# Layer-2 weight, bias and 12 of 16 row tiles loaded inside nucleus step 1, the first group summed and measured in its tail, and the onward stage in another order

## The chip, the cores and the metric

The kernel runs on one core of one Trainium2 chip. The metric is the device time of one execution in microseconds, and lower is better. Engines are named as in the profile: PE (TensorE matmuls), PEld (its weight loads), DVE (VectorE), ACT (ScalarE), POOL (GpSimd) and SP (SyncE, which here only issues DMAs; SPq is its queue).

## What is computed

Four pre-normalised graph layers over 2048 nodes with 256 features, all on one weighted adjacency matrix. The change touches the place between layer 1 and layer 2.

```python
h = relu(layernorm(x));  x = x + L0(h, adj)    # 8-head attention masked and biased by adj
h = relu(layernorm(x));  x = x + L1(h, adj)    # two steps of diffusion and of nucleus (top-p) attention
h = relu(layernorm(x));  x = x + L2(h, adj)    # a_norm @ h @ W.T + b
h = relu(layernorm(x));  x = x + L3(h, adj)    # relu(adj_norm @ (h @ weight))

def L1(X, S, ...):                             # tail of layer 1
    Y = X + Z                                  # Z: the sum of the diffused and attended rows, weighted
    return (Y - mean(Y)) / sqrt(var(Y) + 1e-5) * gamma + beta

def L2(x, adj, W, b):
    deg = adj.sum(axis=1);  dis = (deg + 1e-8) ** -0.5
    return (dis[:, None] * adj * dis[None, :]) @ x @ W.T + b
```

## The kernel before, in words

The rows are held as 16 tiles of 128 partitions by 256 features. The program is a row of phases, written out by hand for each engine: `setup`, `adjacency`, `attend` (layer 0), then for the two steps of layer 1 `refresh` and `nucleus`, then `onward` and `last`. Between two phases stands a barrier of all engines, at which the phase's semaphores are cleared, so the next phase begins when the slowest engine of this one is done. Inside a phase each engine works down its own list and waits on semaphores. Nothing is scheduled by a planner.

`nucleus` for step 1 ends in `last_tiles` on PE: the products of the last four tiles (12 to 15), each followed by `after`, which turns one tile, multiplies it by a weight and adds it into `y` (ACT copies out). Beside this DVE runs the tail: when the first 12 tiles of `y` are ready, it takes `bn_stats` (L2480) and `bn_aggr` (L2483) of each, adds epsilon (L2485), and centres them and multiplies by gamma (L2487). POOL raises the result to the power of minus one half (L2029). SP loads the halves of the transposed adjacency (L1624, L1627) and has nothing left to do after the last of them.

`onward` (L964) makes layer 2's input. Its work goes in four groups ("quads") of four tiles, b = 0 to 3:

- SP loads the saved rows `x_d` (they already hold beta) into `add`, a group at a time (L996), between them layer 2's weight and bias (L998, L999), then layer 3's weight (L1000). It waits until all of that is there and only then issues the 16 loads of the transposed adjacency, 1 MB each (L1005), which `last` reads.
- DVE: `stats_of(0, 3)` measures the four tiles of `y` that the tail left out. `row_scales` makes row factors. `onto(b)` (L1115) multiplies a tile of `y` by its inverse deviation and adds it to `add`: that is x after layer 1. `stats_of(1, b)` (L1096 to L1102) measures it, POOL makes the power (L1014), `aim(b)` (L1122) makes the negative mean times the inverse deviation. `weights_in` (L1133, L1134) copies the turned weight and the broadcast bias out of PSUM. `remainder(b)` (L1128) makes the low halves.
- ACT: `normal(b)` (L1059) is the normalised and rectified group, `copy(b)` (L1066) brings the turned group out of PSUM, `cut(b)` (L1074, L1077) cuts the product into high half and rest. The order is normal(b), copy(b), cut(b-1).
- PE: it turns the weight (L1045) and broadcasts the bias (L1046), then `turn(b)` (L1027, eight transposes) and `products(b)` (L1036). The order is turn(b+1), products(b). Its first instruction waits for `w_loaded` at 48, which counts layer 2's weight, its bias and layer 3's weight.

`last` multiplies the adjacency tiles by the result (L1225) in 16 steps, each waiting for its own tile, then does layer 3 (L1258). The trace leaves numbers out of names: `l_w` is the weight of layer 2 (L1045) and of layer 3 alike, `l_b_row` is `l2_b_row`.

## Time and profile before

| | us |
|---|---|
| median of 3 runs | 3342.86 (3341.6 to 3344.99) |
| the profiled execution | 3342.79 |
| its span in the trace | 3341.0 |
| PE busy in the span | 2956.0 (88%) |
| DVE busy | 2162.7 (65%) |
| ACT busy | 1346.5 (40%) |
| end of `nucleus` step 1 (last ACT result) | 3087.97 |
| `onward`, from DVE's first to its last instruction | 3088.98 to 3147.39 |
| `last`, from PE's first product to the end | 3148.23 to 3341 |

The page sums busy time over the whole span, in which the engines' shares are averages over phases with different limits. For the stretch around the change the timeline of each engine is read instead: each row has the start, the duration from the first to the last of the merged instructions, and in brackets the idle time of the engine ahead of it with what ended it. Single windows of 0.5 us show TensorE's granted clock, as a share of 2.4 GHz.

### The profile page before, as it was taken

The numbers are of one execution on the slowest core, as the hardware profiler recorded it, in microseconds if no ns is written. First come the engines' busy times: TensorE is split into PE (matmuls) and PEld (weight loads), VectorE is DVE, ScalarE is ACT, GpSimd is POOL, SyncE is SP. The second block draws the span as 40 slices with busy tenths as digits, with TensorE's granted clock in tenths as the row PEclk, the third lists the DMA queues.
The fourth block names the chain that finished last, engine by engine and source line by source line (L and its number), as shares of the span: only waits on it lengthen the run. The fifth ranks groups of instructions, "written<-read, shape, count | busy, mean of one in ns | idle before, by whom it ended". The sixth has DMA issues, their size and how long they took to land. (4 is left out here: it accounts for less than half of the span.)

```text
span 3341.0 us, 56511 instructions
## 1 busy us (share of the span) xinstructions
PE 2956.0 (88%) x20632; PEld 2223.5 (67%) x20632; DVE 2162.7 (65%) x4426; ACT 1346.5 (40%) x1750; POOL 57.2 (2%) x70
## 2 busy tenths in 40 slices
PE   3989999999999999999999778878784668697699
PEld 3976776767767677676776447656563556575588
DVE  7866655556555565656556488888488887886331
ACT  5743434444344443344434323333316455522311
POOL 0000000000000000000000000000000000000100
PEclk7999999999999999999999989989987889899899
DMA  7938647466474664746647412100010010100500
GB/s 267 410 134 203 184 120 199 112 190 186 117 201 111 192 183 117 196 120 183 193 112 218 107 57 89 39 13 14 26 40 25 3 49 13 39 26 2 232 1 26
DMA packets 587858, 396.82 MB, mean 119 GB/s; under 512 B 538563, under 2 KB 553414, under 8 KB 562118
## 3 DMA queue, kind: packets, MB, share of 16 engines
q1 hardware_dynamic: 585990, 382.49, 38.5%
q10 hardware_dynamic: 1728, 12.58, 1.1%
q8 instruction: 73, 1.20, 0.1%
q14 instruction: 67, 0.55, 0.1%
HBM read 223.05 MB, written 37.75 MB: 78 GB/s over the span
## 5 line engine op out<-in xcount | busy, mean ns | idle before, releaser
L652 PE MATMUL av<-vw_hi,pT_hi 128*128 128x256 f16 x2048 | 559.7, 273 | 7.4 <-DMA pT_lo<-e_lo 7.4
L805 DVE SCALAR_TENSOR_TENSOR e_lo<-e,e_hi 128x2048 f16<-128x2048 f32 x128 | 293.2, 2291 | 420.7 <-ACT e_hi L716 414.7
L652 PE MATMUL av<-vw_hi,pT_lo 128*128 128x256 f16 x2048 | 559.9, 273 | 0.0
L652 PE MATMUL av<-vw_lo,pT_hi 128*128 128x256 f16 x2048 | 559.8, 273 | 0.0
L641 PE MATMUL logits<-kT_hi,qT_hi 128*128 128x512 f16 x1024 | 388.5, 379 | 0.6 <-DVE vT_lo L825 0.6
L641 PE MATMUL logits<-kT_hi,qT_lo 128*128 128x512 f16 x1024 | 388.1, 379 | 0.0
L641 PE MATMUL logits<-kT_lo,qT_hi 128*128 128x512 f16 x1024 | 388.1, 379 | 0.0
L710 ACT ACTIVATE att_small<-att_small,minus 128x1 f32<-128x1 f32 x128 | 37.6, 294 | 769.5 <-DVE att_small L800 769.5
L791 DVE CUSTOM_DVE_ANT_0 e<-logits,bias,att_small 128x1024 f32<-128x1024 f32 x256 | 328.3, 1282 | 0.6 <-issue 0.3
L2050 DVE SCALAR_TENSOR_TENSOR nuc_junk<-nuc_e,nuc_thr 128x2048 bf16<-128x2048 f32 x140 | 323.7, 2348 | 3.9
L711 ACT ACTIVATE e<-e,att_small,sc 128x2048 f32<-128x2048 f32 x128 | 266.2, 2080 | 0.0
L716 ACT ACTIVATE e_hi<-e 128x2048 f16<-128x2048 f32 x128 | 244.5, 1910 | 16.3 <-DMA pT_hi<-e_hi 1.0
L652 PEld LDWEIGHTS av<-vw_hi,pT_hi 128*128 128x128 f16 x2048 | 201.0, 98 | 44.4 <-issue 8.1
L652 PEld LDWEIGHTS av<-vw_lo,pT_hi 128*128 128x128 f16 x2048 | 200.9, 98 | 36.3
L652 PEld LDWEIGHTS av<-vw_hi,pT_lo 128*128 128x128 f16 x2048 | 200.9, 98 | 23.8
L1707 PE MATMUL nuc_l<-logit_k,logit_q 128*128 128x512 f32 x256 | 134.5, 677 | 64.1 <-ACT nuc_e L1902 57.1
L641 PEld LDWEIGHTS logits<-kT_hi,qT_lo 128*128 (+1 forms) x1024 | 100.2, 98 | 120.9
L641 PEld LDWEIGHTS logits<-kT_hi,qT_hi 128*128 (+1 forms) x1024 | 100.1, 98 | 118.7 <-issue 10.6
L641 PEld LDWEIGHTS logits<-kT_lo,qT_hi 128*128 (+1 forms) x1024 | 100.2, 98 | 106.6
L1683 PE MATMUL nuc_l<-nuc_u,nuc_xsT 128*128 128x256 f32 x320 | 90.6, 439 | 79.9 <-ACT nuc_xsT L1880 69.2
L384 PE MATMUL adj_tp<-ident_one,adj_rows 128*128 128x129 f32 x512 | 123.1, 405 | 30.5 <-DVE adj_count L420 30.5
L384 PEld LDWEIGHTS adj_tp<-ident_one,adj_rows 128*128 128x128 f32 x512 | 122.9, 337 | 30.7 <-DVE adj_count L420 30.7
(436 smaller groups left out, 5783.6 us busy)
## 6 DMA issues: line engine op xcount, KB each, us to landing
bias<-bias_scratch SPq DMA_DIRECT2D x130, 1024.0 KB, 4.8
bias_scratch<-adj_bias SPq DMA_DIRECT2D x16, 1024.0 KB, 8.5
adjT_scratch<-adjT SPq DMA_DIRECT2D x16, 1024.0 KB, 8.7
nuc_at_hi<-adjT_scratch SPq DMA_DIRECT2D x32, 512.0 KB, 3.8
nuc_at_lo<-adjT_scratch SPq DMA_DIRECT2D x32, 512.0 KB, 4.5
adjT<-adjT_scratch SPq DMA_DIRECT2D x16, 1024.0 KB, 20.0
adj_rows<-in_adj_dram ACTq DMA_DIRECT2D x12, 1024.0 KB, 8.9
adj_rows<-in_adj_dram SPq DMA_DIRECT2D x4, 1024.0 KB, 13.7
```

Source lines behind the costliest of these rows:

```text
L384: last = nc.tensor.matmul(o, rows_u[:, t // 2, t % 2 * P:(t % 2 + 1) * P], ident1[:, :], start=True, stop=True)
L641: last = nc.tensor.matmul(o, QT[w][:, k, ds(t * P, P)], KT[x][:, k, c0:c0 + BANK], start=(k == 0 and w == x == 0), stop=(k == 1 and w == 1))
L652: last = nc.tensor.matmul(AV[par], PT[par][w][:, m, :], VW[x][:, m, :], start=(m == 0 and w == x == 0), stop=(m == T - 1 and w == 1))
L710: nc.scalar.activation(masked(par), nb(par), ACT.Exp, bias=minus[:, 0:1], scale=1.0)
L711: nc.scalar.activation(E[par][:, :], E[par][:, :], ACT.Exp, bias=nb(par), scale=sc[:, 0:1], accum_out=ssum(par)).then_inc(exped, 1)
L716: nc.scalar.activation(EH[:, :], E[par][:, :], ACT.Copy, scale=P_SCALE).then_inc(hi_s, 1)
L791: return nc.vector.tensor_tensor_reduce(E[par][:, cols], L[half][:, :], B[par][:, cols], 1.0, (small[:, par, 6:7], m0(par))[half], ALU.add ...
L805: nc.vector.scalar_tensor_tensor(out=EL[:, :], in0=E[par][:, :], scalar=P_SCALE, in1=EH[:, :], op0=ALU.mult, op1=ALU.subtract).then_inc(lo ...
L1683: nc.tensor.matmul(WEIGHTED, xT[:, n * D + k * P:n * D + (k + 1) * P], U[:, n, k, :], start=(n == k == 0), stop=False)
L1707: last = nc.tensor.matmul(scores_in(i)[:, b * BANK:(b + 1) * BANK], QT[:, i * P:(i + 1) * P], KT[:, b * BANK:(b + 1) * BANK], start=True, ...
L2050: nc.vector.scalar_tensor_tensor(out=void[:, k % 2, :], in0=e[:, g % 2, k, 0:N], scalar=bound[:, k:k + 1], in1=e[:, g % 2, k, 0:N], op0=co ...
```

## The change

1. The buffers of layer 1's small weights become views of one tile `wbuf` of the same size, kept outside of the layer-1 block. `x_mv`, `x_rstd` and the semaphores `x_here` and `w2_here` move out too.
2. In `nucleus` step 1 SP, behind its last adjacency load, loads layer 2's weight into `wbuf` and the bias into the row of `gb` that held beta. It then loads the groups 0, 1 and 2 of `x_d`, each when `c_done` says that PE and ACT are done with the four tiles of `acc` that it overwrites.
3. The tail on DVE goes on: the sum of group 0, its statistics and the addition of epsilon. POOL gets a second power instruction.
4. In `onward` SP loads only the fourth group and layer 3's weight and then issues the 16 adjacency loads with no wait between. PE's first wait is for layer 2's weight and bias alone. The copies of `weights_in` move from DVE to ACT. On PE the order becomes products(b), turn(b+1). On ACT cut(b-1) now stands ahead of copy(b). On DVE `aim(0)` comes first, group 1 ahead of the statistics of `y`'s last four tiles and of `row_scales`, and `centre(3)` one group later.

```diff
@@ build
+            wbuf = sb(c, "small_weights", [P, 2 * D])
+            x_mv, x_rstd = sb(c, "x_mv", [P, T, 2]), sb(c, "x_rstd", [P, T])
+            ahead = (wbuf, gb, x_d, x_here, w2_here, x_mv, x_rstd, a["L2_gnn_W"], a["L2_gnn_b"])
@@ nucleus, SP
+                if step:
+                    sp.dma_start(wbuf[:, :].rearrange("p (k n) -> p k n", k=KC), w2_d.rearrange("(k p) n -> p k n", p=P)).then_inc(w2_here, 16)
+                    sp.dma_start(gb[0:1, 1, :], b2_d.rearrange("(a d) -> a d", a=1)).then_inc(w2_here, 16)
+                    for b in range(DONE // 4):
+                        sp.wait_ge(c_done, 4 * (b + 1))
+                        sp.dma_start(out[:, 4 * b:4 * b + 4, :], x_d[:, 4 * b:4 * b + 4, :]).then_inc(x_here[b], 16)
+                    sp.wait_ge(w2_here, 32)
+                    for b in range(DONE // 4):
+                        sp.wait_ge(x_here[b], 16)
@@ nucleus, POOL
+                    pl.wait_ge(x_asked, 1)
+                    nc.gpsimd.tensor_tensor(x_rstd[:, 0:4], x_rstd[:, 0:4], halfp[:, 0:4], ALU.pow).then_inc(tail_powed, 1)
@@ nucleus, DVE, behind the tail
+                    v.wait_ge(tail_powed, 1)
+                    v.wait_ge(x_here[0], 16)
+                    for t in range(4):
+                        nc.vector.scalar_tensor_tensor(out=out[:, t, :], in0=y[:, t, :], scalar=y_rstd[:, t:t + 1], in1=out[:, t, :],
+                                                       op0=ALU.mult, op1=ALU.add).then_inc(x_chain, 1)
+                    for t in range(4):
+                        v.wait_ge(x_chain, 4 + t)
+                        nc.vector.bn_stats(y_stats[:, t, :], out[:, t, :]).then_inc(x_chain, 1)
+                    v.wait_ge(x_chain, 8)
+                    for t in range(4):
+                        nc.vector.bn_aggr(x_mv[:, t, :], y_stats[:, t, :]).then_inc(x_chain, 1)
+                    v.wait_ge(x_chain, 12)
+                    nc.vector.tensor_scalar(x_rstd[:, 0:4], x_mv[:, 0:4, 1], LN_EPS, None, ALU.add).then_inc(x_asked, 1)
@@ onward, PE
-                pe.wait_ge(w_loaded, 48)
+                pe.wait_ge(w2_here, 32)
...
-                pe.wait_ge(copied_w, 2)
                 turn(0)
                 for b in range(QUADS):
+                    if b == 0:
+                        pe.wait_ge(copied_w, 2)
+                    products(b)
                     if b + 1 < QUADS:
                         turn(b + 1)
-                    products(b)
@@ onward, ACT
                 normal(0)
+                weights_in()
                 copy(0)
                 for b in range(1, QUADS):
                     normal(b)
+                    cut(b - 1)
                     copy(b)
-                    cut(b - 1)
```

On DVE, from the centring at the end of `nucleus` step 1 into `onward`, the order was this (`nuc_y_stats`, `deg` and `onw_mv` hold statistics, `acc` is `add`, `l_in` and `l_out` are the row factors, `l_wT` and `l_bias` the copies of `weights_in`):

```order
L2487 SCALAR_TENSOR_TENSOR y<-y,deg,gamma_beta 128x256 x12
L1616 UNCONDITIONAL_BRANCH
L1087 UNCONDITIONAL_BRANCH
L1144 MEMSET l_ones 1x128
L1096 BN_STATS onw_stats<-y 128x6 x4
...
L1142 TENSOR_SCALAR l_out<-l_out 128x16
L1115 SCALAR_TENSOR_TENSOR acc<-y,y_rstd,acc 128x256 x4
L1096 BN_STATS onw_stats<-acc 128x6 x4
L1099 BN_AGGR onw_mv<-onw_stats 128x2 x4
L1102 TENSOR_SCALAR onw_rstd<-onw_mv 128x4
L1133 COPY l_wT<-l_tp 128x512
```

In the changed program the same stretch reads:

```order
L2501 SCALAR_TENSOR_TENSOR y<-y,deg,gamma_beta 128x256 x12
L2507 SCALAR_TENSOR_TENSOR acc<-y,y_rstd,acc 128x256 x4
L2511 BN_STATS nuc_y_stats<-acc 128x6 x4
L2514 BN_AGGR x_mv<-nuc_y_stats 128x2 x4
L2516 TENSOR_SCALAR x_rstd<-x_mv 128x4
L1619 UNCONDITIONAL_BRANCH
L1095 UNCONDITIONAL_BRANCH
L1148 MEMSET l_ones 1x128
L1131 SCALAR_TENSOR_TENSOR onw_minus<-x_mv,x_rstd 128x4
L1123 SCALAR_TENSOR_TENSOR acc<-y,y_rstd,acc 128x256 x4
L1104 BN_STATS onw_stats<-acc 128x6 x4
```

The sum and the statistics of group 0 moved across the phase's end (the two branches), and `onward` begins with the small instruction that ACT's first group waits for.

On ACT, at the start of `onward`, the order was this (`y` is the normalised group, `onw_xT` the turned one, `h_hi` and `onw_rest` the cut product):

```order
L1059 ACTIVATE y<-acc,onw_minus,onw_rstd 128x256 x4
L1066 ACTIVATE onw_xT<-onw_tp 128x512 x2
L1059 ACTIVATE y<-acc,onw_minus,onw_rstd 128x256 x4
L1066 ACTIVATE onw_xT<-onw_tp 128x512 x2
L1074 ACTIVATE h_hi<-onw_u,l_in 128x256
L1077 ACTIVATE onw_rest<-onw_u,l_in 128x256
```

It now is:

```order
L1061 ACTIVATE y<-acc,onw_minus,x_rstd 128x256 x4
L1083 ACTIVATE l_wT<-l_tp 128x512
L1084 ACTIVATE l_bias<-l_bc 128x256
L1068 ACTIVATE onw_xT<-onw_tp 128x512 x2
L1061 ACTIVATE y<-acc,onw_minus,x_rstd 128x256 x4
L1076 ACTIVATE h_hi<-onw_u,l_in 128x256
L1079 ACTIVATE onw_rest<-onw_u,l_in 128x256
```

The two copies of the weight and the bias came in, and the second `onw_xT` moved behind the eight cuts.

On PE, in `onward`, the order of the transposes (`onw_tp`) and the products (`onw_u`) was:

```order
L1045 MATMUL l_tp<-ident,l_w 128x128 x4
L1046 MATMUL l_bc<-l_b_row,l_ones 128x256
L1027 MATMUL onw_tp<-ident,y 128x128 x16
L1036 MATMUL onw_u<-l_wT,onw_xT 128x256 x8
L1027 MATMUL onw_tp<-ident,y 128x128 x8
L1036 MATMUL onw_u<-l_wT,onw_xT 128x256 x8
L1027 MATMUL onw_tp<-ident,y 128x128 x8
L1036 MATMUL onw_u<-l_wT,onw_xT 128x256 x16
```

and is now:

```order
L1046 MATMUL l_tp<-ident,small_weights 128x128 x4
L1047 MATMUL l_bc<-gamma_beta,l_ones 128x256
L1028 MATMUL onw_tp<-ident,y 128x128 x8
L1037 MATMUL onw_u<-l_wT,onw_xT 128x256 x8
L1028 MATMUL onw_tp<-ident,y 128x128 x8
L1037 MATMUL onw_u<-l_wT,onw_xT 128x256 x8
```

followed by the same pair twice more. Each group's products no longer stand behind the next group's transposes.

## Rows read from the trace of the kernel before

**Rows 1.** The chain that ended last: start us, us, what.
```profile
3148.23 31.60 PE last_pr L1225 x288
...
3337.43 0.42 DVE acc L1342
```
**Rows 2.** Windows: us, busy by engine (count), granted clock, DMA share, GB/s.
```profile
3160.00:3341.00 181.00, 176.88 (x1558) 158.10 (x1556) 38.43 (x98) 26.51 (x56) 9.56 (x12) 1.00 0.04 13
```
**Rows 3.** Waits 3060 to 3160: engine, line, waited for: total us, times, longest.
```profile
ACT y L1059 <- DVE onw_minus L1122: 18.0, 4, 16.7
...
PE l_tp L1045 <- DMA l_w<-in_L_gnn_weight_dram: 11.9, 1, 11.9
```
**Rows 4.** DVE's timeline, end of `nucleus` and `onward`.
```profile
3080.28 4.83 DVE L2487 SCALAR_TENSOR_TENSOR y<-y,deg,gamma_beta 128x256 f32<-128x256 f32 x12
3088.98 0.17 DVE L1144 MEMSET l_ones<- 1x128 f32 x1 [3.87 <-PEq L127]
...
3091.82 0.17 DVE L1142 TENSOR_SCALAR l_out<-l_out 128x16 f32<-128x16 f32 x1
...
3102.74 1.66 DVE L1115 SCALAR_TENSOR_TENSOR acc<-y,y_rstd,acc 128x256 f32<-128x256 f32 x4
...
3104.51 1.40 DVE L1096 BATCH_NORM_STATS2 onw_stats<-acc 128x6 f32<-128x256 f32 x4
...
3106.36 0.17 DVE L1102 TENSOR_SCALAR onw_rstd<-onw_mv 128x4 f32<-128x4 f32 x1
...
3146.97 0.42 DVE L1128 SCALAR_TENSOR_TENSOR h_lo<-h_hi,onw_rest 128x256 f16<-128x256 f16 x1 [0.30 <-ACT onw_rest L1077]
```
**Rows 5.** ACT's timeline, end of `nucleus` and `onward`.
```profile
3087.59 0.38 ACT L1939 ACTIVATE y<-nuc_l 128x256 f32<-128x256 f32 x1 [1.65 <-PE nuc_l L1780]
3104.63 2.07 ACT L1059 ACTIVATE y<-acc,onw_minus,onw_rstd 128x256 f32<-128x256 f32 x4 [16.66 <-DVE onw_minus L1122]
3108.83 1.08 ACT L1066 ACTIVATE onw_xT<-onw_tp 128x512 f32<-128x512 f32 x2 [2.12 <-PE onw_tp L1027]
...
3143.64 0.47 ACT L1074 ACTIVATE h_hi<-onw_u,l_in 128x256 f16<-128x256 f32 x1 [2.15 <-PE onw_u L1036]
...
3146.45 0.48 ACT L1077 ACTIVATE onw_rest<-onw_u,l_in 128x256 f32<-128x256 f32 x1
```
**Rows 6.** PE's timeline in `onward`.
```profile
3099.50 1.12 PE L1045 MATMUL l_tp<-ident,l_w 128*128 128x128 f32 x4 [11.95 <-DMA l_w<-in_L_gnn_weight_dram]
3100.55 1.22 PE L1046 MATMUL l_bc<-l_b_row,l_ones 1*128 1x256 f32 x2
3106.85 1.94 PE L1027 MATMUL onw_tp<-ident,y 128*128 128x128 f32 x8 [5.09 <-ACT y L1059]
...
3114.00 4.90 PE L1036 MATMUL onw_u<-l_wT,onw_xT 128*128 128x256 f32 x16
...
3141.63 3.69 PE L1036 MATMUL onw_u<-l_wT,onw_xT 128*128 128x256 f32 x16 [1.75 <-ACT onw_rest L1077]
```
**Rows 7.** POOL's timeline: one power instruction of `onward`.
```profile
3097.57 1.01 POOL L1014 TENSOR_TENSOR onw_rstd<-onw_rstd,halfp 128x4 f32<-128x4 f32 x1 [5.45 <-DVE onw_rstd L1102]
```
**Rows 8.** DVE's timeline in `last`: statistics that wait for the instruction before.
```profile
3154.71 0.43 DVE L1316 BATCH_NORM_STATS2 l_stats<-acc 128x6 f32<-128x256 f32 x1
3155.17 0.18 DVE L1317 BATCH_NORM_AGGREGATE l_mv<-l_stats 128x2 f32<-128x6 f32 x1
```
**Rows 9.** Windows of 0.5 us in which the granted clock changes.
```profile
3092.50:3093.00 0.50, 0.00 (x0) 0.00 (x0) 0.00 (x0) 0.00 (x0) 0.00 (x0) 0.68 0.94 332
...
3116.50:3117.00 0.50, 0.50 (x3) 0.39 (x2) 0.00 (x0) 0.00 (x0) 0.00 (x0) 0.93 0.93 393
```
**Rows 10.** The 16 adjacency loads: issue ns min/median/max, first and last start; landing.
```profile
L1005 SPq DMA_DIRECT2D adjT<-adjT_scratch x16: 333/500/2390, 3099.5 to 3114.3; - x16
...
DMA to landing us min/median/max: 4.8/20.0/27.2
```
**Rows 11.** The page's groups: DVE's masked sums of both nucleus steps.
```profile
L2050 DVE SCALAR_TENSOR_TENSOR nuc_junk<-nuc_e,nuc_thr 128x2048 bf16<-128x2048 f32 x140 | 323.7, 2348 | 3.9
```

More of the change, by code:

```diff
@@ L178, in build @@
                           ([a["L1_gnn_U1"][step], a["L1_gnn_U2"][step]] + [a["L1_gnn_U3"][0], a["L1_gnn_U3"][1]] * step, at_d, scales, ident16, Y, sc,
-                           Xp, Xf, Xb, step), (w1, w2, w3), (gb, halfp, row_stats, y_rstd))
+                           Xp, Xf, Xb, step), (w1, w2, w3), (gb, halfp, row_stats, y_rstd), ahead)
             AT = sb(c, "adjT", [P, T, 2, T, P], F16)
@@ L183, in build @@
             Hq = [sb(c, f"h_{n}", [P, T, D], F16) for n in ("hi", "lo")]
-            phase(onward, a, Y, acc, x_d, at_d, AT, at_here, ident, halfp, gb, row_stats, y_rstd, scales, wtop, W3, bb, l2_out, l3_in, l3_out, Hq)
+            phase(onward, a, Y, acc, ahead, at_d, AT, at_here, ident, halfp, gb, row_stats, y_rstd, scales, wtop, W3, bb, l2_out, l3_in, l3_out, Hq)
             phase(last, AT, at_here, ident, ident16, halfp, W3, bb, acc, Y, Hq, l2_out, l3_in, l3_out, out)
-        nc.clear_and_free_semaphores(at_here + rows_here)
+        nc.clear_and_free_semaphores(at_here + rows_here + x_here + [w2_here])
 def adjacency_rows(adj):
@@ L961, in _, with onward @@
                 statistics(T - 1)
-def onward(nc, sb, ps, sem, a, src, add, shifted_d, at_d, AT, at_here, ident, halfp, gb, row_stats, y_rstd, scales, wtop, W3, bb, l2_out, l3_in, l3_out, Hq):
-    w_loaded, turned_w, copied_w, rows_done, one = (sem("onw_" + s) for s in ("w_loaded", "turned_w", "copied_w", "rows", "one"))
-    x_here = [sem(f"onw_x_here{b}") for b in range(4)]
+def onward(nc, sb, ps, sem, a, src, add, ahead, at_d, AT, at_here, ident, halfp, gb, row_stats, y_rstd, scales, wtop, W3, bb, l2_out, l3_in, l3_out, Hq):
+    wbuf, _, shifted_d, x_here, w2_here, x_mv, x_rstd, _, _ = ahead
+    w3_here, turned_w, copied_w, rows_done, one = (sem("onw_" + s) for s in ("w3_here", "turned_w", "copied_w", "rows", "one"))
     asked, powed, aimed, made, tp_s, xt_s, prod_s, cut_s, lo_s, dve = (
@@ L971, in onward @@
     QUADS = T // QUAD
-    ASKS = ((0, 3), (1, 0), (1, 1), (1, 2), (1, 3))
+    ASKS = ((1, 1), (0, 3), (1, 2), (1, 3))
     CENTRED = QUADS - 1
     with ExitStack() as c:
-        w2, wT = sb(c, "l2_w", [P, KC, D]), sb(c, "l2_wT", [P, KC, D])
-        row, ones = sb(c, "l2_b_row", [1, D]), sb(c, "l2_ones", [1, P])
+        w2, wT = wbuf[:, :].rearrange("p (k n) -> p k n", k=KC), sb(c, "l2_wT", [P, KC, D])
+        row, ones = gb[0:1, 1, :], sb(c, "l2_ones", [1, P])
         l2_in = sb(c, "l2_in", [P, 2, T])
-        stats, x_mv = sb(c, "onw_stats", [P, T, 6]), sb(c, "onw_mv", [P, T, 2])
-        x_rstd, minus = sb(c, "onw_rstd", [P, T]), sb(c, "onw_minus", [P, T])
+        stats = sb(c, "onw_stats", [P, T, 6])
+        minus = sb(c, "onw_minus", [P, T])
         mv, rstd = (row_stats, x_mv), (y_rstd, x_rstd)
@@ L1077, in cut, with weights_in @@
                         nc.scalar.activation(rest[:, t % QUAD, :], product_of(t), ACT.Copy, scale=l2_in[:, 1, t:t + 1]).then_inc(cut_s, 1)
+                def weights_in():
+                    s.wait_ge(turned_w, 1)
+                    nc.scalar.activation(wT[:, :, :].rearrange("p k d -> p (k d)"), w_tp[:, :], ACT.Copy).then_inc(copied_w, 1)
+                    nc.scalar.activation(bb[:, :], bc[:, :], ACT.Copy).then_inc(copied_w, 1)
                 normal(0)
+                weights_in()
                 copy(0)
@@ L1144, in _ @@
                 nc.vector.memset(ones[:, :], 1.0).then_inc(one, 1)
+                aim(0)
+                onto(1)
+                stats_of(1, 1)
                 stats_of(0, 3)
                 row_scales()
-                onto(0)
-                stats_of(1, 0)
-                weights_in()
-                onto(1)
-                aim(0)
-                stats_of(1, 1)
+                aim(1)
+                onto(2)
+                stats_of(1, 2)
                 centre(3)
-                onto(2)
-                aim(1)
-                stats_of(1, 2)
                 remainder(0)
@@ L1534, in _, with nucleus @@
                         nc.vector.tensor_copy(QT[:, b * BANK:(b + 1) * BANK], TP[b // 2][b % 2][:, :]).then_inc(w2_read, 1)
-def nucleus(nc, sb, ps, sem, name, QT, KT, parts, out, ident, diffusion, next_logits, tail):
+def nucleus(nc, sb, ps, sem, name, QT, KT, parts, out, ident, diffusion, next_logits, tail, ahead):
     weights, at_d, scales, ident16, y, sc, Xp, Xf, Xb, step = diffusion
@@ L1558, in nucleus @@
     gb, halfp, row_stats, y_rstd = tail
+    wbuf, _, x_d, x_here, w2_here, x_mv, x_rstd, w2_d, b2_d = ahead
+    (x_asked, x_chain) = (sem(f"{name}_x_{s}") for s in ("asked", "chain"))
     DONE = T - G
```

27 lines of the change are left out of this document (11 added, 16 removed).

## The prediction, made before the changed kernel had been run

> **What bounds the kernel now.** I read the chain of waits first. It ends in an unbroken run of PE work through `last`, from 3148.23 to the last DVE addition at 3337.43 [rows 1], and the window over that phase shows PE busy 176.88 of 181 us at a granted clock of 1.00, which is 2.4 GHz [rows 2]. So `last` takes as long as its products take, and what the change can give is an earlier start of `last`. That start is set by `onward` and by the barrier behind it. The reader should see next that `onward` is not bound by any engine's work. ACT's longest wait is 16.7 us for DVE's `onw_minus`, and PE waits 11.9 us for a weight [rows 3]. The weight that ended it is layer 3's, which `onward` never multiplies by: PE's first wait counts it, and it stands in SP's queue behind all four groups of rows. PE therefore turns layer 2's weight only at 3099.50 [rows 6], DVE copies it out behind that, sums group 1 from 3102.74 [rows 4] and only then makes the factor for which ACT starts its first group, at 3104.63 [rows 5]. The phase began at 3088.98 [rows 4]. Thus the first products come at 3114.00 [rows 6], 25.0 us into a phase of 58.4 us (3088.98 to 3147.39).
>
> **The tail of nucleus step 1.** DVE ends its centring at 3080.28 + 4.83 = 3085.11 [rows 4], and ACT ends the phase at 3087.59 + 0.38 = 3087.97 [rows 5], so DVE has 2.86 us to spare. The change adds: four sums, 1.66 us as in `onward`'s row [rows 4]; four `bn_stats`, each of which now waits for the one before, at 0.46 us from start to start [rows 8] = 1.84 us, against 1.40 us for four in a pipeline [rows 4]; four `bn_aggr` and the epsilon, 3104.51 + 1.40 = 3105.91 to 3106.53, 0.62 us [rows 4], with some 0.05 us for handing over twice more. DVE ends near 3085.11 + 0.02 + 1.66 + 0.03 + 1.84 + 0.62 = 3089.3. POOL then needs 1.01 us [rows 7], with 0.05 us for the hand-over as an estimate, so POOL closes the phase at 3090.36, **2.4 us later** than ACT did. This is the one cost on the path. Taking the pipelined figure for the statistics gives 2.0 us; a POOL that is slow in passing the barrier could make it 3. The first instruction of `onward` moves from 3088.98 to 3091.4.
>
> **The loads in nucleus step 1.** SP issues them behind its last adjacency load. For groups 0 and 1 the condition was met long before; group 2 waits for the twelfth tile, which is ready ahead of `last_tiles`. Three groups of 0.5 MB and 0.25 MB of weight are small beside the 16 MB that land within 42 us in `onward` [rows 10], and SP has nothing behind them there but waits for their landing. DVE's search and PE's products of that time read no DMA. I cost this at nothing; the cover is DVE's work up to 3085.
>
> **The start of onward.** With the factor made at once, counting from DVE's first instruction: the weight and bias on PE end at 0.2 + 2.27 = 2.5 us (3099.50 to 3100.55 + 1.22) [rows 6]; ACT's first group ends at 0.3 + 2.07 = 2.4 us [rows 5]; the eight transposes take 1.94 us [rows 6] to 4.45, and ACT's copies 1.08 us [rows 5] to 5.6. The weight's two copies on ACT stand in the time of the transposes. Their cost, not shown on ACT, is bounded by the same 1.08 us for two such reads of PSUM, and ACT is free from 2.5 to 4.5. So products(0) begin at **5.6 us instead of 25.0**.
>
> **What is late next.** Group 1. DVE makes its factor behind one `onto` (1.69 us), one `stats_of` (2.0 us, 3104.51 to 3106.53) and the statistics of `y` with the row scales, 3.0 us (3088.98 to 3091.99) [rows 4]: at 6.9 us. ACT's normal(1) then ends at 9.0. cut(0) is eight activations at about 0.365 us (3143.64 to 3146.93 for eight, 3.3 us, holds a wait for the second half of the products; 0.365 is my estimate without it) [rows 5], to 12.0. The new order puts copy(1) behind it, to 13.2, where products(1) start. I take products(0) as off the path: with 3.69 or 4.90 us [rows 6] they end ahead of 12.0.
>
> **The repeating part.** In the last group products start at 3141.63 [rows 6], ACT's first cut follows at 3143.64 and the last ends at 3146.93 [rows 5], 5.3 us after the start. In the new order copy(b+1) comes next, 1.08 us and 0.1 us of handing over: **6.5 us from products to products**. normal(b+1) fits into ACT's 2.0 us ahead of the first cut, since its factor is made right behind remainder(b-1), while ACT copies. The transposes, on PE behind the products, are over before the last cut ends. So products(2) start at 19.7, products(3) at 26.2, and the last `h_lo` ends 5.76 us later (3141.63 to 3147.39) [rows 4, 6]: 31.9 us.
>
> **TensorE's clock.** At 3092.5 to 3093 it fell to 1.2 GHz, some five microseconds after the last products of the tail, with PE idle all the while,, and it came back to 2.4 GHz within 3116.5 to 3117, during the products that followed transposes [rows 9]. That is why one group of products took 4.90 us and the last one 3.69 [rows 6]. After the change PE's idle time at the barrier is about 4 us instead of 12, and between groups some 2 us. I expect a low clock at the start and perhaps once more, and put in 4.90 - 3.69 = 1.2 us for one group on the path: onward becomes **33.1 us**.
>
> **The sum.** `last` starts 0.84 us behind the end of `onward` (3147.39 to 3148.23) [rows 1, 4]. New: 3091.4 + 33.1 + 0.84 = 3125.3, against 3148.23: **22.9 us earlier**. `last` keeps its length, since its products fill it. The span of 3341.0 becomes 3318.1. The profiled execution took 3342.79, 1.8 us more than its span and 0.07 below the median, so the time is **3319.9 us**.
>
> **The adjacency loads.** SP now issues them from about 1 us into `onward`, near 3092.4 instead of 3099.5 [rows 10], so the last lands 7.1 us before 3114.3 + 27.2 = 3141.5, at 3134.4. `last` starts at 3125.3, while some are under way, where before all had landed. The shortest landing was 4.8 us [rows 10], so the first tile is there by 3098. A step of `last` takes 48 products, 31.60 x 48/288 = 5.27 us [rows 1], and tiles arrive every 2.6 us (42 us over 16). PE uses them more slowly than they come, so I cost this at nothing. The fourth group of rows is first in that queue and isn't needed for 14 us.
>
> **Rivals.**
>
> A. The clock stays at 1.2 GHz through `onward`, because its products stand too thinly. Products would then take up to 3.69 x 2 less a fixed end, 6.9 us as an estimate, and eight transposes the 1.94 us seen [rows 6]. Then a group takes 10.0 us: 5.6, 15.6, 25.6, 35.6, and the end 44.5 us. `last` starts at 3136.7, a gain of 11.5: 3331.3. Against it: even before, with PE waiting 5.09 us for a group, the clock came back in each group of products [rows 6, 9].
>
> B. The adjacency loads are late for `last`, if its first tile in fact lands with the last ones. PE then starts at 3134.4 + 0.5, a gain of 13.3: 3329.5. The 4.8 us minimum [rows 10] speaks against it.
>
> C. Only the first group's products run wholly at 1.2 GHz, because the transposes and the wait ahead of them leave the clock low: 5.6 + 6.9 + 1.94 + 1.1 puts products(1) at 15.6 instead of 13.2. With this in place of the 1.2 us above the time is 3321.1. For it: 2.27 us of transposes and bias ahead of a wait did not bring the clock back at 3101.8 [rows 6, 9]. Against it: at 3116.5 it came back some 2.5 us into the products, and transposes were all that PE had done right ahead of them.
>
> The Trainium skill ("TensorE: Matmul & The Clock Gate", section "Part 4: PE-mode transpose") says that transposes don't count as a busy TensorE for the clock. By that rule C is what happens.
>
> D. The change doesn't hide the loads: the rows land after DVE reaches the new sum, so that the tail waits. For this the last of 1.75 MB would have to take until 3085, though group 2 is asked for ahead of `last_tiles`. It would cost the wait one to one; a wait of 17 us would make the change unmeasurable (3336). I see no row for it.
>
> E. Slower than before. `x_mv` and `x_rstd` (192 bytes per partition) now lie ahead of all buffers of the two nucleus steps, which moves every one of them. If DVE's long instructions depended on where their operands lie, its search would slow: 140 of one kind at 2348 ns [rows 11]. To turn 22.9 us of gain into a loss of 6.7 they must cost 29.6/140 = 0.21 us more each, 9%. At 10% the time is 3319.9 + 32.4 = 3352. The group reads four tiles at four addresses in each step and its count times its mean is its whole time, so no slow address stands out; I give it little.
>
> **How the numbers follow.** The forecast, with none to two groups at a low clock: 0.68. C: 0.18. A: 0.06. B: 0.03. D: 0.02. E: 0.02. Others 0.01, slower. The forecast's own spread: without the clock's 1.2 us and with pipelined statistics 3318.2, and the runs shown spread by about 1.5 us around their median, so 3317 below. Above, two groups wholly at the low clock cost 2 x 3.5 us over the all-fast 3318.7, and a slower barrier another microsecond: 3327. A measurement of this kernel can tell about 0.2%, 6.7 us, from no change. A, B and C are gains beyond that. Faster 0.94, within 0.2% 0.03, slower 0.03.
>
> **What the profile after would show.** DVE's tail ends near 3089.3 and POOL's second power near 3090.4. PE's first wait of 11.9 us is gone, ACT's 16.7 us too. Products start near 5.6, 13.2, 19.7 and 26.2 us into `onward`, with ACT almost without a gap from the second group on. `last` starts near 3125 and lasts as long as before, with no wait for `adjT`. A wait of DVE for `acc<-x_scratch` in the tail would speak for D, products(1) at 15.6 for C, a start of `last` at 3137 with a clock of 0.50 throughout for A, a mean of L2050 over 2.5 us for E. The sum is wrong if ACT's order makes group 1 later than 13.2, or if POOL's closing of the phase costs more than its instruction.

## The result and the profile after

| | before | after |
|---|---|---|
| median | 3342.23 us (4 runs, 3341.42 to 3344.99) | 3321.3 us (4 runs, 3316.91 to 3323.81) |
| the profiled execution, and its span | 3342.79, 3341.0 | 3321.59, 3319.8 |
| `onward`, DVE's first to last instruction | 58.41 | 31.99 |
| start of `last` | 3148.23 | 3125.50 |

The ratio is 0.9935, with a 95% interval of 0.9917 to 0.9952. The prediction was 3319.9 us, with a range of 3317.0 to 3327.0.

The chain of waits of the changed kernel, its first piece in `last` and its last piece (start us, us, what), beside [rows 1]:

```profile
3125.50 33.12 PE last_pr L1226 x288
...
3316.21 0.42 DVE acc L1343
```

It is still one run of PE work to the end. But 288 products that took 31.60 us now take 33.12 us. Next come the waits between 3060 and 3160 (total us, times, longest), which answer to [rows 3]:

```profile
ACT y L1061 <- DVE onw_minus L1131: 5.1, 3, 3.7
PE l_tp L1046 <- DVE l_ones L1148: 4.2, 1, 4.2
```

The waits of 16.7 and 11.9 us are gone, and what is left of both is the barrier between the phases. The timelines of the changed kernel answer to [rows 4 to 7] (start us, us, engine, line, what, and in brackets the idle time ahead). DVE's, with POOL's power and ACT's two rows below it:

```profile
3081.55 4.84 DVE L2501 SCALAR_TENSOR_TENSOR y<-y,deg,gamma_beta 128x256 f32<-128x256 f32 x12
3086.42 1.67 DVE L2507 SCALAR_TENSOR_TENSOR acc<-y,y_rstd,acc 128x256 f32<-128x256 f32 x4
3088.12 1.81 DVE L2511 BATCH_NORM_STATS2 nuc_y_stats<-acc 128x6 f32<-128x256 f32 x4
3089.97 0.38 DVE L2514 BATCH_NORM_AGGREGATE x_mv<-nuc_y_stats 128x2 f32<-128x6 f32 x4
3090.39 0.17 DVE L2516 TENSOR_SCALAR x_rstd<-x_mv 128x4 f32<-128x4 f32 x1
3092.70 0.17 DVE L1148 MEMSET l_ones<- 1x128 f32 x1 [2.15 <-PEq L127]
...
3124.26 0.43 DVE L1137 SCALAR_TENSOR_TENSOR h_lo<-h_hi,onw_rest 128x256 f16<-128x256 f16 x1 [0.31 <-ACT onw_rest L1079]
...
3090.64 1.01 POOL L2043 TENSOR_TENSOR x_rstd<-x_rstd,halfp 128x4 f32<-128x4 f32 x1 [6.42 <-DVE x_rstd L2516]
...
3088.85 0.39 ACT L1951 ACTIVATE y<-nuc_l 128x256 f32<-128x256 f32 x1 [1.65 <-PE nuc_l L1792]
3092.93 2.09 ACT L1061 ACTIVATE y<-acc,onw_minus,x_rstd 128x256 f32<-128x256 f32 x4 [3.69 <-DVE onw_minus L1131]
```

PE's, the weight's transposes, the first group's and the four groups of products:

```profile
3093.01 1.09 PE L1046 MATMUL l_tp<-ident,small_weights 128*128 128x128 f32 x4 [4.20 <-DVE l_ones L1148]
...
3095.18 1.97 PE L1028 MATMUL onw_tp<-ident,y 128*128 128x128 f32 x8
3098.41 5.13 PE L1037 MATMUL onw_u<-l_wT,onw_xT 128*128 128x256 f32 x16 [1.27 <-ACT onw_xT L1068]
...
3106.18 3.72 PE L1037 MATMUL onw_u<-l_wT,onw_xT 128*128 128x256 f32 x16 [1.76 <-ACT onw_xT L1068]
...
3112.54 3.72 PE L1037 MATMUL onw_u<-l_wT,onw_xT 128*128 128x256 f32 x16 [1.76 <-ACT onw_xT L1068]
...
3118.90 3.72 PE L1037 MATMUL onw_u<-l_wT,onw_xT 128*128 128x256 f32 x16 [1.76 <-ACT onw_xT L1068]
```

POOL ends at 3091.65, 2.41 us behind ACT's last result at 3089.24, and `onward` starts 3.46 us behind that result instead of 1.01: the tail costs 2.45 us. The products stand 5.71, 13.48, 19.84 and 26.20 us into `onward`.

**Where 21.2 us of span went.** I count from one instruction that both kernels have, DVE's last copy to `nuc_ask` in the last group's search of `nucleus` step 1. It stands at 3001.26 before and 2999.74 after. In the fourteen profiles of this study it lies anywhere from 2991.4 to 3001.3 us. The programs up to there differ in next to nothing, and two profiles of the changed kernel itself have it 3.1 us apart (2999.74 and 2996.63). So I count 1.5 us of the 21.2 to that run and not to the change. From this mark on:

| stretch | before | after | gain |
|---|---|---|---|
| the mark to the start of `onward` | 87.72 | 92.96 | -5.24 |
| `onward` | 58.41 | 31.99 | 26.42 |
| barrier | 0.84 | 0.81 | 0.03 |
| `last` | 192.77 | 194.30 | -1.53 |
| from the mark to the end | 339.7 | 320.1 | 19.7 |

The tail is 2.45 us of the 5.24. The rest has no term in the prediction's sum, and the mark is where it begins. DVE's timeline of the kernel before:

```profile
3001.26 0.16 DVE L2309 COPY nuc_ask<-nuc_small 128x4 f32<-128x4 f32 x1
3008.21 0.87 DVE L2219 TENSOR_SCALAR nuc_listed<-nuc_eight,nuc_small 128x8 f32<-128x8 f32 x4 [6.79 <-issue]
```

and of the changed kernel:

```profile
2999.74 0.16 DVE L2323 COPY nuc_ask<-nuc_small 128x4 f32<-128x4 f32 x1
3008.93 0.87 DVE L2233 TENSOR_SCALAR nuc_listed<-nuc_eight,nuc_small 128x8 f32<-128x8 f32 x4 [9.02 <-issue]
```

In this gap DVE only evaluates four branches that skip a loop each. It grew by 2.23 us, and it stands 2 us behind the first new load (SP issues it at 2997.65). The same gap two groups of tiles earlier hardly differs (6.62 before, 6.55 after). The four branches themselves, by their line (duration ns, first and last start), in the kernel before:

```profile
L2248 DVEq COMPARE_BRANCH  x4: 56/56/72, 3002.6 to 3006.8; - x4
```

and in the changed one:

```profile
L2262 DVEq COMPARE_BRANCH  x4: 56/56/72, 3001.1 to 3007.5; - x4
```

Each lasts 56 to 72 ns, but they stretch over 6.4 us instead of 4.2. And the DMA queues (packets, MB, share of the 16 engines) in the 4 us from the mark on, in the kernel before:

```profile
q1 hardware_dynamic: 101, 0.35, 23.9%
q14 instruction: 1, 0.01, 1.5%
```

and in the changed one:

```profile
q1 hardware_dynamic: 502, 1.12, 87.2%
```

Before, a packet of instructions came in these 4 us. After, none did: the new loads fill the same 16 engines, and the packet comes later. The Trainium skill ("Advanced Engine Details and Errata", section "ISA Cache") says that an engine's instruction cache has only two lines, of 16 KB each. The trace agrees in part: over the whole execution queue q8 moves 1.20 MB of instructions in 73 packets, 16 KB each, but q14 moves 0.55 MB in 67, half of that. Which queue serves which engine is not in the trace, so that the late packet is one of DVE's is argued and not shown.

### The profile page after: what moved, and what is told of

The parts are those of the page before. It is cut to its first block and busy times, and to the rows that moved or that the text cites. A ratio compares the mean times of both kernels' runs of the same rounds, so it can differ in the third digit from the quotient of the medians.

```text
span 3319.8 us, 56511 instructions
## 1 busy us (share of the span) xinstructions
PE 2948.3 (89%) x20632; PEld 2216.5 (67%) x20632; DVE 2162.3 (65%) x4424; ACT 1349.1 (41%) x1752; POOL 57.4 (2%) x70
## 5 line engine op out<-in xcount | busy, mean ns | idle before, releaser
L2064 DVE SCALAR_TENSOR_TENSOR nuc_junk<-nuc_e,nuc_thr 128x2048 bf16<-128x2048 f32 x140 | 323.7, 2349 | 3.9
L647 PEld LDWEIGHTS logits<-kT_hi,qT_hi 128*128 (+1 forms) x1024 | 100.1, 98 | 120.2 <-issue 11.9
L1719 PEld LDWEIGHTS nuc_l<-logit_k,logit_q 128*128 128x128 f32 x256 | 53.7, 218 | 134.4 <-issue 67.7
```

Source lines behind the costliest of these rows:

```text
L647: last = nc.tensor.matmul(o, QT[w][:, k, ds(t * P, P)], KT[x][:, k, c0:c0 + BANK], start=(k == 0 and w == x == 0), stop=(k == 1 and w == 1))
L1719: last = nc.tensor.matmul(scores_in(i)[:, b * BANK:(b + 1) * BANK], QT[:, i * P:(i + 1) * P], KT[:, b * BANK:(b + 1) * BANK], start=True, ...
L2064: nc.vector.scalar_tensor_tensor(out=void[:, k % 2, :], in0=e[:, g % 2, k, 0:N], scalar=bound[:, k:k + 1], in1=e[:, g % 2, k, 0:N], op0=co ...
```

## Experiments

Theory: the loads, the tail and the order gain 26.4 us in `onward`, and the loads cost DVE 2.2 us because instruction packets queue behind them. Rivals: one of the parts does nothing; the 2.2 us come from where code lies or from the run; the clock, not the order, sets `onward`. In this section "the mark to `onward`" is read as in the table above (before 87.72, after 92.96), and "first 32" is the time of the first 32 products of `last`, 3.65 us before and 5.17 after.

**Layer 3's weight out of the first wait alone** (on the kernel before):

```diff
-sp.dma_start(W3...).then_inc(w_loaded, 16)
-sp.wait_ge(w_loaded, 48)
+sp.dma_start(W3...).then_inc(w3_here, 16)
+sp.wait_ge(w_loaded, 32)
+sp.wait_ge(w3_here, 16)
...
-                pe.wait_ge(w_loaded, 48)
+                pe.wait_ge(w_loaded, 32)
```

> The kernel before, with layer 3's weight on a semaphore of its own, so that PE's first wait counts layer 2's weight and bias only. The loads, the orders and the tail stay. Theory 1 (the start of onward is a chain of waits, and layer 3's weight behind all row groups ends one of them): PE turns the weight near 3.5 to 6 us after DVE's first instruction instead of 10.5, DVE copies it out right behind the first statistics, and last starts about 4 us earlier: 3338. Theory 2 (what the change gains comes from the new orders and from the loads being gone, that wait being covered by DVE's wait for the rows): under 1 us, 3342.

Measured: 3338.49 us, ratio 0.9997 (0.9986 to 1.0007). `onward` takes 54.50 us, the mark to it 87.73. PE's timeline:

```profile
3090.11 1.12 PE L1047 MATMUL l_tp<-ident,l_w 128*128 128x128 f32 x4 [7.48 <-DMA l_b_row<-in_L_gnn_b_dram]
```

The wait passes on to layer 2's bias, which stands in the same queue. The 11.9 us of [rows 3] were worth 3.9 us of `onward`. The time doesn't show them: its interval holds 1. In this profile `last` began at a low clock (first 32 products 5.04 us) and was 1.3 us longer than before, so that from the mark to the end only 2.6 us are left.

**The loads alone.** Against the changed kernel it has the kernel before's order on all engines of `onward`, `weights_in` back on DVE, and no sum or statistics of group 0 in the tail. What is left of the change is SP's part and PE's first wait:

```diff
@@ onward, ACT
                 normal(0)
-                weights_in()
                 copy(0)
```

> The changed kernel with only its loads: weight, bias and three groups of rows loaded in nucleus step 1, the adjacency loads issued at once. No sum in the tail, and in onward the orders of DVE, ACT and PE as in the kernel before. Theory 1: group 0 is normalised at 9.7 us instead of 15.6, onward lasts some 52.5 us instead of 58.4, and last starts 6 us earlier; time 3336 to 3338 (2 us of it may be lost in nucleus step 1 to the loads). Theory 2 (loads are most of the gain): onward under 45 us, time near 3328.

Measured: 3335.59 us, ratio 0.9983 (0.9973 to 0.9993). `onward` 52.30 us, the gap behind the mark 8.31 and the mark to `onward` 89.96, which is 2.24 more than before with no tail in it. More than a third of the 6.1 us gained in `onward` is thus lost ahead of it.

**Without the tail:**

```diff
@@ nucleus, POOL
-                    pl.wait_ge(x_asked, 1)
-                    nc.gpsimd.tensor_tensor(x_rstd[:, 0:4], x_rstd[:, 0:4], halfp[:, 0:4], ALU.pow).then_inc(tail_powed, 1)
@@ nucleus, DVE: likewise from v.wait_ge(tail_powed, 1) to the epsilon
...
@@ onward, DVE
                 nc.vector.memset(ones[:, :], 1.0).then_inc(one, 1)
+                onto(0)
+                stats_of(1, 0)
-                aim(0)
                 onto(1)
+                aim(0)
```

> The changed kernel without the sum and statistics of group 0 in the tail and without POOL's second power; they stand at the head of onward. Theory 1: the phase boundary comes 2.4 us earlier, ACT's first group starts at 5 us instead of 0.2, products(1) at 16.7 instead of 13.5, and onward lasts 35.2 us instead of 32.0: about 1 us slower in sum, 3322. Rival: the tail costs more than it brings, and this is faster than the changed kernel, 3319.

Measured: 3324.19 us, ratio 0.9952 (0.9936 to 0.9968). `onward` starts 1.01 us behind ACT's last result, as before, and takes 37.56 us, where 35.2 was expected. PE's timeline:

```profile
3095.72 1.97 PE L1028 MATMUL onw_tp<-ident,y 128*128 128x128 f32 x8 [6.18 <-ACT y L1061]
3098.95 5.44 PE L1037 MATMUL onw_u<-l_wT,onw_xT 128*128 128x256 f32 x16 [1.27 <-ACT onw_xT L1068]
```

The tail costs 2.45 us and saves 37.56 - 31.99 = 5.57 us in `onward`, 3.1 us net. The mark to `onward` is 90.62, so 2.9 us of the 5.24 are there without the tail.

**The old orders of PE and ACT:**

```diff
@@ PE
                 for b in range(QUADS):
+                    if b + 1 < QUADS:
+                        turn(b + 1)
...
                     products(b)
-                    if b + 1 < QUADS:
-                        turn(b + 1)
@@ ACT
                     normal(b)
-                    cut(b - 1)
                     copy(b)
+                    cut(b - 1)
```

> The changed kernel with the old order of two engines in onward: PE turns group b+1 ahead of the products of group b, ACT copies the turned group ahead of the cuts. Loads, tail and DVE's order as changed. Theory 1 (the order sets the period of a group, 6.4 us new against 9.7 to 10.7 old): onward lasts about 42 us instead of 32, time 3331. Rival (the chain of waits at the start is all, and the order moves little): onward 34 us or less, time 3323.

Measured: 3330.92 us, ratio 0.9971 (0.9958 to 0.9984). `onward` 43.05 us against 31.99. PE's timeline:

```profile
3101.45 1.97 PE L1028 MATMUL onw_tp<-ident,y 128*128 128x128 f32 x8 [4.52 <-ACT y L1061]
3103.22 4.27 PE L1037 MATMUL onw_u<-l_wT,onw_xT 128*128 128x256 f32 x16
3111.79 1.97 PE L1028 MATMUL onw_tp<-ident,y 128*128 128x128 f32 x8 [4.30 <-ACT y L1061]
3113.55 4.22 PE L1037 MATMUL onw_u<-l_wT,onw_xT 128*128 128x256 f32 x16
```

`onward` starts at 3092.50 here, so products(0) come 10.72 us into it instead of 5.71: they stand behind the second group's transposes, which wait 4.52 us for ACT. That is 5.0 us of the 11.1. From there to products(1) and on to products(2) it takes 10.3 us each, instead of 7.77 and 6.36, with a wait of 4.30 us in each; the last step, with no further group to turn, takes 5.95. This is the largest part that a run shows. PE's and ACT's order were changed together, so their shares are open.

Singly the loads come to 6.1 us of `onward`, the tail to 5.6 and this order to 11.1, together 22.8 of the 26.4. The first was added to the kernel before, the other two were taken out of the changed one, so the sum is only a rough one. DVE's order and the weight's copies on ACT were never switched alone, and the remaining 3.6 us have no run.

**The loads asked for behind the twelfth tile:**

```diff
                 if step:
+                    sp.wait_ge(c_done, DONE)
                     sp.dma_start(wbuf[:, :]...
```

> The changed kernel in which SP waits in nucleus step 1 until all 12 tiles are done with (c_done at 12) before it issues weight, bias and the three groups of rows, instead of issuing weight, bias and two groups some 35 us earlier. Theory (data loads in flight delay DVE where it jumps over code that it skips, because its instructions come over the same DMA engines): DVE's gap between the copies to nuc_ask and the lists of the last four tiles, 6.8 us before and 9.0 us in the changed kernel, returns to 6.8 us, and the kernel is 2.2 us faster, 3319 on a chip where the changed one takes 3321. Rival (the gap grew for another reason, such as moved buffers or the next load's place in the code): the gap stays at 8.3 to 9.1 us and the time with it.

Measured: 3320.26 us, ratio 0.9942 (0.9929 to 0.9956). The timelines of DVE at the gap and of PE at its first products:

```profile
3002.90 0.87 DVE L2234 TENSOR_SCALAR nuc_listed<-nuc_eight,nuc_small 128x8 f32<-128x8 f32 x4 [6.62 <-issue]
...
3091.90 6.70 PE L1037 MATMUL onw_u<-l_wT,onw_xT 128*128 128x256 f32 x16 [1.26 <-ACT onw_xT L1068]
```

and its DMA queues in the 4 us from the mark on:

```profile
q1 hardware_dynamic: 83, 0.27, 18.7%
q14 instruction: 1, 0.01, 1.4%
```

One added wait on SP takes the gap back to 6.62 us and the packet of instructions back into the first 4 us. The mark to `onward` is 90.19: 87.72 and the tail's 2.45, to 0.02 us. So the unforeseen 2.8 us came from loads under way this early. All profiles agree. I take from the mark to `onward` what the phase's end lies later behind ACT's last result: the nine with early loads are then 2.2 to 3.5 us longer than before, the three with late loads 0 to 0.3. In this profile the first group's products ran wholly at the low clock, which is the prediction's case C, and `onward` took 33.41 us. The 2.2 us that I expected in the time are not seen there: the ratio lies between those of the changed kernel's two measurements (0.9935 and 0.9951).

**1 MB of DMA more at the same place:**

```diff
+                    sp.dma_start(extra_d[:, 0:8, :], x_d[:, 0:8, :]).then_inc(extra_s, 16)
                     for b in range(DONE // 4):
...
+                    sp.wait_ge(extra_s, 16)
```

> The changed kernel with 1 MB more of copying from memory to memory, issued by SP in nucleus step 1 ahead of the rows of groups 0 and 1; its data is not used. Theory (loads in flight delay DVE's skipping jumps): the gap of 9.0 us grows, by up to the 3 to 5 us for which the transfers last longer, to 11 to 14 us. Rival: it stays at 9.0 us.

One run, 3321.58 us. The branches stretch from 2998.9 to 3005.9, 7.0 us, and DVE's gap is:

```profile
3008.11 0.87 DVE L2237 TENSOR_SCALAR nuc_listed<-nuc_eight,nuc_small 128x8 f32<-128x8 f32 x4 [10.35 <-issue]
```

The gap grows again, by less than I had expected (11 to 14). Over all profiles it is 6.62 to 7.47 us where no new load is under way there (before, the first experiment, and three with late loads), 8.31 to 9.71 with the loads (eight profiles), and 10.35 with the extra copy. This one profile lies only 0.64 us above the highest of the eight, so that more data delays more is weakly supported.

**Group 0 ahead of the last four centrings of the tail:**

```diff
-                    for t in range(DONE):
+                    for t in range(DONE - G):
                         nc.vector.scalar_tensor_tensor(out=y[:, t, :], ...
...
+                    for t in range(DONE - G, DONE):
+                        nc.vector.scalar_tensor_tensor(out=y[:, t, :], ...
```

> The changed kernel with the tail in another order: DVE centres tiles 0 to 7, then sums and measures group 0 and asks POOL for the power, and centres tiles 8 to 11 while POOL works. Expected by the reading that POOL's power closes the phase: DVE ends the tail at 8.7 us behind the start of the centring and POOL has long ended, where POOL ended 10.1 us behind it, so onward starts 1.4 us earlier; the kernel is 1 to 1.5 us faster. Rival (the barrier, not POOL, sets it, or DVE must wait for the first power of 12 columns): no difference.

Measured: 3319.4 us, ratio 0.9939 (0.9925 to 0.9952). The timelines of POOL and of DVE at the phase's end:

```profile
3083.22 1.18 POOL L2043 TENSOR_TENSOR x_rstd<-x_rstd,halfp 128x4 f32<-128x4 f32 x1 [4.84 <-DVE x_rstd L2516]
...
3083.05 1.67 DVE L2518 SCALAR_TENSOR_TENSOR y<-y,deg,gamma_beta 128x256 f32<-128x256 f32 x4
3085.97 0.17 DVE L1148 MEMSET l_ones<- 1x128 f32 x1 [1.25 <-PEq L127]
```

`onward` starts 2.57 us behind ACT's last result instead of 3.46: 0.9 us saved, where 1.4 was expected. POOL is out of the way, but DVE now ends at 3084.72 and closes the phase, and the barrier takes 1.25 us behind DVE. The time shows none of it (0.9939 beside 0.9935).

**Transposes as filler for the clock**, 16 on PE at the end of `onward` and 24 at the end of `nucleus` step 1, which nobody reads:

```diff
+                for n in range(16):
+                    nc.tensor.transpose(TP[0][n % 2][:, 0:P], ident[:, :], ident[:, :])
...
+                        for n in range(24):
+                            nc.tensor.transpose(L[0][:, n % 2 * BANK:n % 2 * BANK + P], ident[:, :], ident[:, :])
```

> The changed kernel with transposes of the identity on PE, whose results nobody reads, in its two idle stretches: 24 behind the last tile of nucleus step 1 and 16 behind the last products of onward. Theory (PE's idle time at the two barriers lets the clock fall, for which the start of onward and of last pay): the clock stays at 2.4 GHz from the tail of nucleus step 1 into last, products(0) take 3.7 us instead of 5.1, the first 288 products of last take 31.6 us instead of 33.1, and the kernel is 1.5 to 2 us faster. Rival (transposes don't count as activity): the clock falls as before and nothing is gained.

Measured: 3319.68 us, ratio 0.9941 (0.9928 to 0.9955). PE's timeline:

```profile
3094.41 5.22 PE L1037 MATMUL onw_u<-l_wT,onw_xT 128*128 128x256 f32 x16 [1.26 <-ACT onw_xT L1070]
...
3118.53 1.91 PE L1056 MATMUL onw_tp<-ident 128*128 128x128 f32 x16
3121.57 3.65 PE L1228 MATMUL last_pr<-h_hi,adjT 128*128 128x256 f16 x32 [1.13 <-PEq L127]
```

The filler at `onward`'s end keeps the first 32 at 3.65 us, and `last` is 192.73 us long. The one in the tail doesn't help the first group's products (5.22), though the weight's transposes right behind the barrier take 0.63 us instead of 1.09.

**Products as filler**, eight and six of them:

```diff
+                for n in range(8):
+                    nc.tensor.matmul(TP[0][n % 2][:, 0:D], ident[:, :], w2[:, 0, :], start=True, stop=True)
...
+                        for n in range(6):
+                            nc.tensor.matmul(L[0][:, n % 2 * BANK:n % 2 * BANK + D], ident[:, :], U[:, 0, 0, :], start=True, stop=True)
```

> The changed kernel with products that nobody reads in place of the sixteen and twenty-four transposes of the run with filler: eight products of 128x256 on PE at onward's end (some 1.8 us) and six behind the last tile of nucleus step 1 (some 1.4 us). The tail's filler ends ahead of POOL, so it costs no time by itself. Theory 1 (transposes don't count for the clock, products do): the clock is now held over the barrier, so that products(0) take 3.7 us instead of 5.1 to 5.2 and the transposes of the weight and of the first group stay at 1.00; onward 30.6 us. Theory 2 (filler of either kind counts alike, and the tail's filler was too early or too short to matter): products(0) again 5 to 5.5 us, onward 32 us. In both the first 32 products of last take 3.65 us, as with transposes. Time 3318 by theory 1, 3319.5 by theory 2.

Measured: 3322.62 us, ratio 0.9948 (0.9935 to 0.9962). PE's timeline:

```profile
3080.54 2.75 PE L1838 MATMUL nuc_l<-nuc_u,ident 128*128 128x256 f32 x12
3084.90 0.63 PE L1046 MATMUL l_tp<-ident,small_weights 128*128 128x128 f32 x4 [1.61 <-DVE l_ones L1150]
...
3090.18 5.13 PE L1037 MATMUL onw_u<-l_wT,onw_xT 128*128 128x256 f32 x16 [1.27 <-ACT onw_xT L1070]
...
3114.20 3.62 PE L1056 MATMUL onw_tp<-small_weights,ident 128*128 128x256 f32 x16
3118.61 3.65 PE L1228 MATMUL last_pr<-h_hi,adjT 128*128 128x256 f16 x32 [0.79 <-PEq L127]
```

and two windows of it of 2 us (granted clock is the third number from the right):

```profile
3084.00:3086.00 2.00, 1.10 (x6) 0.71 (x6) 1.41 (x6) 1.19 (x3) 0.00 (x0) 1.00 0.19 47
3086.00:3088.00 2.00, 1.21 (x6) 1.06 (x6) 1.93 (x7) 1.64 (x4) 0.00 (x0) 0.57 0.84 230
```

Theory 1 falls: PE was busy with products to 3083.29, and products(0) still took 5.13 us. The clock did stay at 1.00 over the barrier (the weight's transposes took 0.63 us instead of 1.09), but it fell in the second of these windows, near 3086.3, while PE waited for ACT's first group. Nor is the filler shown to be what kept it up: the profile with late loads has no filler, PE idle for 4.20 us, and 0.63 us for the same transposes. The eight products take 3.62 us, twice what I had put down (they run as sixteen passes), so PE now closes the phase. `last` starts 2.19 us behind DVE's end instead of 0.81. That costs 1.4 us of the 1.5 that the clock gives.

**Late loads, group 0 early and the products as filler**; then **the same without filler**; then **the changed kernel again**, all on one chip. Their diffs are those shown above.

> The changed kernel with four edits: the loads asked for only behind the twelfth tile, group 0 summed and measured ahead of the centring of the last four tiles, and the two fillers of products. My terms: late loads give back 2.2 us, the earlier power 0.9 us, the filler at onward's end 1.5 us, against the changed kernel on the same chip: 4.6 us less, ratio to before 0.9925. The gap of DVE behind nuc_ask is 6.6 to 7.0 us, onward starts 2.4 to 2.6 us behind ACT's end, last's first 32 products take 3.65 us. If the loads' delay was not the cause of the gap, or if it is made up elsewhere, only 2.4 us less.

> The same as the run ahead of it without both fillers: late loads and earlier power alone. Expected 3.1 us less than the changed kernel on the same chip. The clock falls at the barriers as it does in the changed kernel: first 32 products of last 5.2 us, where the run ahead has 3.65.

> The changed kernel itself on the chip of the three runs ahead of it, for a comparison on one chip. Expected ratio to before 0.9935, gap of DVE behind nuc_ask 9 us, onward 32.0 us or, where the clock comes back only after the first group's products, 33.3 us.

| | median us (5 runs) | ratio to before | mark to `onward` | `onward` | first 32 | mark to end |
|---|---|---|---|---|---|---|
| with filler | 3319.68 | 0.9940 (0.9926 to 0.9953) | 90.14 | 33.40 | 3.65 | 318.5 |
| without | 3314.69 | 0.9928 (0.9914 to 0.9942) | 89.60 | 31.91 | 5.21 | 316.6 |
| changed, again | 3321.70 | 0.9951 (0.9937 to 0.9964) | 93.40 | 33.56 | 5.32 | 322.2 |

The version without filler is the fastest of the study. Its five runs (3310.54 to 3317.31) all lie below the five of the changed kernel (3320.64 to 3325.03), 7.0 us by the medians where I expected 3.1. From the mark to the end it is 5.6 us shorter: 3.8 from the loads and the tail, 1.65 from the clock in `onward`, which can't be put down to the edits: products(0) took 5.20 us against 6.71, and they differ as much between two executions of the changed kernel. A further 4.5 us between these two profiles lie ahead of the mark, where their programs do the same. Of the 5.0 us by which the version with filler is behind, the profiles from the mark on explain 1.9, and 1.5 of those are the clock in `onward`; the rest I can't assign. The changed kernel's PE timeline in the last of these runs:

```profile
3095.74 6.71 PE L1037 MATMUL onw_u<-l_wT,onw_xT 128*128 128x256 f32 x16 [1.27 <-ACT onw_xT L1068]
...
3105.09 3.72 PE L1037 MATMUL onw_u<-l_wT,onw_xT 128*128 128x256 f32 x16 [1.76 <-ACT onw_xT L1068]
```

Products(0) took 5.13 us in the first profile of this kernel and 6.71 in this one, with the second group 15.06 us into `onward`, as case C has it. So the forecast and C are not two outcomes of the kernel but two of its executions: of the ten profiles with the new order, six have 5.13 to 5.53 us and four 6.55 to 6.71.

## Why the prediction was right, point by point

- **What bounds.** Right. `last` is one chain of PE work, and its start moved by 22.73 us for the predicted 22.9 (1.5 us of that lies ahead of the mark).
- **The tail.** 2.45 us for 2.4. Its instructions took 1.67, 1.81 and 0.59 us where 1.66, 1.84 and 0.62 were put down, and POOL closed the phase with 1.01.
- **The loads in nucleus step 1.** This step failed. They were costed at nothing, because "DVE's search and PE's products of that time read no DMA". DVE reads no rows by DMA there and was still late with them: 2.2 us directly behind the mark, and 2.8 us by the start of `onward`. That its instructions come by DMA is the reading that fits, not a thing that a run switched. The named cover, DVE's work up to 3085, was the very thing delayed.
- **The start of onward.** 5.71 us for 5.6. ACT's copies of the weight and bias took 0.98 us and cost nothing, as said.
- **What is late next, and the repeating part.** 13.48 for 13.2, then 6.36 us from products to products for 6.5. Without the term for the clock the sum said 31.9 us, measured 31.99.
- **TensorE's clock.** The 1.2 us for one group were put in the wrong place. The first group did run low (5.13 us against 3.72), but ACT was busy with normal(1) meanwhile, so nothing of it stood on the path in this execution; wholly low (6.71 us, where case C put down 6.9) it costs 1.6 us (33.56). Before the change the prediction read some five idle microseconds of PE ahead of the clock's fall. After it the clock fell within 3091.0 to 3091.5, some 2.3 us behind PE's last product of the tail (3088.81). The loss came in `last`: the clock fell while PE stood idle for 2.88 us behind `onward`'s products. Single windows of the changed kernel (granted clock is the third number from the right):

```profile
3123.50:3124.50 1.00, 0.00 (x0) 0.00 (x0) 0.66 (x2) 0.73 (x2) 0.00 (x0) 1.00 0.98 410
3124.50:3125.50 1.00, 0.00 (x0) 0.03 (x1) 0.19 (x1) 0.00 (x0) 0.01 (x1) 0.86 1.02 426
3125.50:3126.50 1.00, 1.00 (x5) 0.69 (x6) 0.00 (x0) 0.00 (x0) 1.00 (x2) 0.50 1.00 418
...
3128.50:3129.50 1.00, 1.00 (x10) 0.86 (x9) 0.00 (x0) 0.00 (x0) 1.00 (x2) 0.93 1.02 410
```

  The first 3.1 us of `last` at 1.2 GHz cost 1.5 us. "`last` keeps its length" was wrong by that.
- **The adjacency loads.** Right. `last` has no wait for `adjT`, with the 16 loads issued from 3093.5 and landing in 7.4 to 28.5 us.
- **The rivals.** A, B and D didn't happen: the clock came back in the first group, no tile was late, and DVE has no wait for `x_scratch` in the tail. E did not either: the group of L2050 (now L2064) has a mean of 2349 ns, 2348 before. (The prediction's argument against E, that the count times the mean is the whole time, holds for every group and says nothing.) C happens in four of ten profiles.
- **The sum.** 3319.9 for 3321.3. That it came out so close is in part luck, because errors offset: 2.8 us of loads and 1.5 us in `last` were missing, against 1.2 us of clock charged in `onward` and 1.5 us that the profiled run had gained ahead of the mark.

## What to carry to other kernels

An engine that reads no data by DMA can still be delayed by bulk loads: here DVE was, by 2.2 to 3.5 us, where it skipped loops. Look for "instruction" queues in the trace, and ask for bulk loads no earlier than they are needed. When a phase is bound by a hand-over between engines, write down the order of one period on each engine: here products that stood behind another group's transposes cost 5.0 us at the start and 2.6 and 3.9 us in the next two periods, while the wait of 11.9 us in the list of waits was worth only 3.9 us. Compare stages from a common mark, since profiles of programs that are alike up to there had it up to 10 us apart, and two of the very same program 3.1 us.
